# An adaLN block of a two-way Mamba scan and nine experts: downs turned to channel by time, GpSimd's product a slot later, and slots respread

## What is computed

```python
mod = silu(c) @ wmod                       # six rows per batch: sa, ca, ga, sb, cb, gb
h   = layernorm(x) * (1 + ca) + sa
x1  = x + ga * (h + mamba_f(norm(h)) + flip(mamba_b(flip(norm(h)))))
h2  = layernorm(x1) * (1 + cb) + sb
out = x1 + gb * (sum_e w[:, e] * swiglu_e(h2) + swiglu_shared(h2))   # 8 experts, two chosen, softmax of the two

def mamba(xn):                             # 256 inner channels, 16 states
    u, z = split(xn @ Win.T); u = silu(conv4(u)); dt, B, C = project(u)
    h = exp(dt * A) * h + (dt * u) * B     # along time, for each state
    y = sum over states of h * C + u * D
    return (y * silu(z)) @ Wout.T
swiglu_e(t) = (silu(t @ w1) * (t @ w2)) @ w3     # 256 hidden channels
```

## Time and profile before

| | us |
|---|---|
| median of 3 runs | 2398.07 |
| the runs | 2397.0 to 2398.93 |
| the profiled execution's own time | 2398.73 |
| its span, from first to last instruction | 2396.9 |

### The profile page before, as it was taken

One profiled execution on the slowest core, in us unless ns is written; L12 is line 12 of the kernel. 1 busy time (PEld: TensorE's weight loads), 2 busy tenths in 40 slices (PEclk: granted clock), 3 DMA queues, 4 the chain that ended last, 5 costly groups with the idle time before them and its releaser, 6 DMA issues. The chain is left out here.

```text
span 2396.9 us, 31820 instructions
## 1 busy us (share of the span) xinstructions
PE 2026.4 (85%) x9957; PEld 1283.8 (54%) x9957; DVE 2236.7 (93%) x3546; ACT 1504.6 (63%) x2483; POOL 2021.7 (84%) x1334
## 2 busy tenths in 40 slices
PE   6678988879798888988889798888988888897868
PEld 2445655545565555555545465555555555455544
DVE  4999999999999999999999999999999999999962
ACT  4656666676666666666666666666666666666633
POOL 2777989989898998989989898998989889897855
PEclk7688999999999898999999999998999999999999
DMA  5333433433343333334433343343433333343310
GB/s 148 138 137 124 148 130 128 144 130 136 129 147 134 121 138 134 142 126 145 137 127 132 133 142 134 134 141 118 142 134 140 131 133 137 126 138 131 137 59 27
DMA packets 124060, 312.41 MB, mean 130 GB/s; under 512 B 19700, under 2 KB 46308, under 8 KB 123892
## 3 DMA queue, kind: packets, MB, share of 16 engines
q1 hardware_dynamic: 123892, 310.39, 37.5%
HBM read 303.74 MB, written 6.60 MB: 129 GB/s over the span
## 5 line engine op out<-in xcount | busy, mean ns | idle before, releaser
L504 POOL TENSOR_TENSOR bt<-v,bb 128x1024 f32<-128x1024 f32 x511 | 1205.3, 2360 | 93.8 <-DVE psA L942 72.4
L942 DVE TENSOR_TENSOR_SCAN psA<-psA,bt 128x512 f32<-128x512 f32 x1024 | 1198.1, 1217 | 49.3 <-ACT psA L689 42.4
L689 ACT ACTIVATE psA<-dt,aneg 128x512 f32<-128x512 f32 x1024 | 688.4, 688 | 685.2 <-DVE g L952 684.0
L1209 PEld LDWEIGHTS psY<-ident,g 128*128 128x128 f32 x4096 | 491.6, 147 | 504.5 <-DVE g L952 281.2
L1209 PE MATMUL psY<-ident,g 128*128 128x128 f32 x4096 | 590.1, 286 | 198.1 <-DVE g L952 197.9
L952 DVE TENSOR_TENSOR g<-psA,cb 128x512 f32<-128x512 f32 x1024 | 675.0, 679 | 0.0
L602 POOL TENSOR_TENSOR act<-pf,gf 128x512 f32<-128x512 f32 x288 | 366.8, 1274 | 112.2 <-DVE pf L1046 90.7
L1318 PE MATMUL F<-h2T,w 128*128 128x512 f32 x576 | 334.0, 664 | 112.4 <-DVE pf L1046 110.7
L1364 PE MATMUL F<-w,act 128*128 128x128 f32 x2304 | 298.0, 276 | 4.4 <-POOL act L602 3.1
L1364 PEld LDWEIGHTS F<-w,act 128*128 128x128 f32 x2304 | 276.7, 192 | 14.8 <-POOL act L602 11.0
L1225 PE MATMUL psP<-xnT,wcT 128*128 128x512 f32 x496 | 238.6, 604 | 0.0
(11 more groups left out here) (184 smaller groups left out, 1922.5 us busy)
## 6 DMA issues: line engine op xcount, KB each, us to landing
bb<-bc_rows SPq DMA_DIRECT2D x256, 512.0 KB, 3.7
cb<-bc_rows SPq DMA_DIRECT2D x256, 512.0 KB, 3.6
wB<-w_rows SPq DMA_DIRECT2D x80, 256.0 KB, 4.1
x<-in_L_attn_x SPq DMA_DIRECT2D x16, 256.0 KB, 4.4
out_x<-osb SPq DMA_DIRECT2D x16, 256.0 KB, 4.3
modA<-mod_table SPq DMA_DIRECT2D x15, 192.0 KB, 4.1
w<-in_L_ffn_ew SPq DMA_DIRECT2D x2, 1024.0 KB, 7.2
bc_rows<-xd SPq DMA_DIRECT2D x32, 64.0 KB, 3.0
```

What stands on the lines that cost most here:

```text
L504: g.tensor_tensor(bt[:, n % 2, :, :], v[d][:, :, :], bb[:, n // 2 % 2, n % 2, :].unsqueeze(1).broadcast_to([P, NH, T]), ALU.mult).then_inc ...
L689: s.activation(psA[:, half * T:half * T + T], dt_[d][:, half, :], ACT.Exp, scale=aneg[d][:, half, n:n + 1]).then_inc(a_s, 1)
L942: w.tensor_tensor_scan(ah, ah, bt[:, n % 2, half, :][:, order], 0.0, ALU.mult, ALU.add)\
L1209: last = m.matmul(psY[:, half * T + i * P:half * T + i * P + P], g_[:, n % 2, half, i * P:i * P + P], ident[:, :], is_transpose=True, star ...
```

## The change

- **Downs.** Each is now one pair of passes with 512 columns: `w3` is stationary, the activation streams, and the result is channel by time. The order of the experts is 0, 1, shared, 2 to 7. Experts 0 and 1 come out separately; DVE multiplies each by its row of weights and the batch's gate (`product`, slots 14 and 16, into `apart`). The other seven, of which six have scaled inputs, add up in one group in `F2`.
- **End of a batch's experts.** In slot 0 of the body after, ACT copies the group out with the gate (`fold`, ahead of `keep_y`); PE transposes the two products and the folded group into `F1` (`final_turn`, slots 0 and 1); DVE adds the residual (`output`, slot 2). POOL's `output`, ACT's copy, DVE's `expert_sum`, and the two copies of the routing's scores are gone; the routing reads its scores from PSUM.
- **POOL's product** `act` is two slots behind the up instead of one (`ACT_LAG`), into six half buffers instead of three pairs. The ups move to end in slot 29, the downs in slot 31. `make_v` backward moves from slot 14 to 12, the two products of the first layernorm from 7 to 4, the routing weights two slots earlier.
- **Rows of weights**: three buffers, eight rows a batch, written in slot 10 and read from slot 11; in SP's list they come ahead of that slot's rows for the scan.
- **Skip, z.** The forward direction's skip goes into `psY` in slots 8 and 12, and the turns back are plain transposes. The four z parts lie in slots 31, 2, 3 and 5 (PE and ACT) and 0, 3, 4 and 6 (DVE), where they were in 29 to 31 and 2 to 6.

The diff's core:

```diff
-V_SLOT = (30, 14)
-Z_SLOTS, ZS_SLOTS = ((29, 30), (2, 5)), ((30, 31), (6, 6))
+V_SLOT = (30, 12)
+Z_SLOTS = {2: (1, 0), 3: (0, 1), 5: (1, 1)}
+Z_AHEAD_SLOT = 31
+ZS_SLOTS = {0: (0, 0), 3: (1, 0), 4: (0, 1), 6: (1, 1)}
+SKIP_SLOTS = (8, 12)
-UP_SLOTS = [slot for slot in range(7, 28) if slot not in (9, 10, 22)]
-DOWN_SLOTS = [10, 11, 14, 15, 16, 17, 18, 19, 20, 21, 22, 24, 29, 29, 30, 30, 31, 31]
+UP_SLOTS = [slot for slot in range(7, 30) if slot not in (9, 10, 20, 22, 28)]
+DOWN_SLOTS = [10, 11, 15, 16, 17, 18, 21, 24, 25, 26, 27, 28, 28, 29, 29, 30, 31, 31]
+ACTS = 6
+ACT_LAG = 2
-TURN_SLOT, ROWS_SLOT = 13, 14
-XS_SLOTS = {16: 4, 18: 5, 20: 6, 22: 7, 24: 8}
+TURN_SLOT = 10
+XS_SLOTS = {14: 3, 16: 4, 18: 5, 21: 6, 24: 7, 26: 8}
+FOLD_SLOT, FINAL_SLOT, OUT_SLOT = 0, 1, 2
...
-                k = up_at(slot - 1)
+                k = up_at(slot - ACT_LAG)
...
+            def fold(fb):
+
+                act_e.wait_ge(down_s, UPS * fb + UPS)
+                s.activation(foT, F2[:, :], ACT.Copy, scale=modC[:, 2:3]).then_inc(F2_free, 1)
...
+                    if slot == FOLD_SLOT and b >= 2:
+                        fold(b - 2)
                     if slot == 0 and ffn:
                         keep_y(b - 1, 1)
...
+            def product(fb, p):
+
+                n = NX * fb + p
+                dve.wait_ge(down_s, UPS * fb + 2 * p + 2)
+                dve.wait_ge(wB_in[n % ROWS], 16 * (n // ROWS) + 16)
+                wait(dve, fin_s, fb)
+                w.scalar_tensor_tensor(apart[:, p, :], F2[:, :], modC[:, 2:3], wB[:, n % ROWS, :],
+                                       ALU.mult, ALU.mult).then_inc(F2_free, 1)
...
+            def final_turn(fb, slot):
+
+                if slot == FINAL_SLOT - 1:
+                    pe.wait_ge(F1_free, UPS * fb + UPS)
+                    pe.wait_ge(F2_free, FREES * fb + DOWN + APART)
+                    for p in range(APART):
+                        for i in range(NT):
+                            m.matmul(F1[:, i * P:i * P + P], apart[:, p, i * P:i * P + P], ident[:, :],
+                                     is_transpose=True, start=(p == 0 and i == 0), stop=False, skip_group_check=True)
...
-                for e, part in downs_at(slot):
-                    if part == 0:
-                        pe.wait_ge(act_s, 2 * NE * fb + 2 * e + 2)
...
+                for k in downs_at(slot):
+                    if k <= 2 * APART and k % 2 == 0:
+                        pe.wait_ge(F2_free, free + DOWN + k // 2)
+                    pe.wait_ge(act_s, UPS * fb + k + 1)
+                    m.matmul(F2[:, :], w3[:, ORDER[k // 2], k % 2, :], act[:, k % ACTS, :],
+                             start=(k <= 2 * APART and k % 2 == 0), stop=(k < 2 * APART and k % 2 == 1 or k == UPS - 1))\
+                        .then_inc(down_s, 1)
```

More of the change, by code:

```diff
@@ L74, in downs_at, with z_order, row_expert @@
 def downs_at(slot):
-    return [divmod(k, 2) for k, at in enumerate(DOWN_SLOTS) if at == slot]
-ORDER = [NX] + list(range(NX))
+    return [k for k, at in enumerate(DOWN_SLOTS) if at == slot]
+def z_order(b, d, half):
+    return 4 * b + 2 * d + half if b == 0 else 4 * b + d + 2 * half
+def row_expert(idx):
+    return ORDER[idx if idx < APART else idx + 1]
 def adaln_mamba_moe(nc, t, out):
@@ L291, in adaln_mamba_moe @@
         wrow_out = sem("wrow_out")
-        wB_in = [sem(f"wB_in{k}") for k in range(2)]
+        wB_in = [sem(f"wB_in{k}") for k in range(ROWS)]
         xs_s = sem("xs_s")
@@ L433, in body, with scale_row @@
                         sp.dma_start(modG[:, :], row).then_inc(modG_in, 16)
-                    if slot == 0 and not (isinstance(b, int) and b < 2):
+                    if slot == OUT_SLOT + 1 and b >= 2:
                         store(b - 2)
[L437 to L442, removed]
+            def scale_row(fb, idx):
+                n = NX * fb + idx
+                if n >= ROWS:
+                    done, k = divmod(n - ROWS, NX)
+                    if k < APART:
+                        sp.wait_ge(F2_free, FREES * done + DOWN + k + 1)
+                    else:
+                        sp.wait_ge(xs_s, NS * done + k - APART + 1)
+                row = w_dram[row_expert(idx):row_expert(idx) + 1, :].broadcast_to([P, T])
+                sp.dma_start(wB[:, n % ROWS, :], row).then_inc(wB_in[n % ROWS], 16)
             def scales(fb, slot):
-                if slot == ROWS_SLOT:
+                if slot == ROWS_OUT_SLOT:
                     wait(sp, xs_s, NS * fb)
@@ L449, in scales @@
                     sp.dma_start(w_dram, wtsT[:, :]).then_inc(wrow_out, 16)
[L450 to L456, removed]
+                for idx, at in ROW_SLOTS.items():
+                    if slot == at:
+                        if idx == 0:
+                            sp.wait_ge(wrow_out, 16 * fb + 16)
+                        scale_row(fb, idx)
             def early(b, scan, ffn, last):
@@ L460, in early @@
                     fb = b - 1
[L461 to L466, removed]
+                    wait(sp, F2_free, FREES * fb)
+                    with nc.allow_non_contiguous_dma(reason="three columns"):
+                        sp.dma_start(modC[:, :], mod_dram[bass.ds(fb, 1), 3 * D:6 * D]
+                                     .rearrange("a (k p) -> p (a k)", p=P)).then_inc(modC_in, 16)
                 if scan and not last:
@@ L861, in body @@
                         keep_y(b, 0)
+                    if ffn and slot == GATE_SLOT + 1:
+                        act_e.wait_ge(gate_s, GATES * (b - 1) + GATE_D)
+                        s.activation(ge[:, :], gd[:, :], ACT.Exp).then_inc(ge_s, 1)
                     if ffn:
@@ L885, in _ @@
             passes(act_e, body)
+            fold(NB - 1)
         @block.vector
@@ L1082, in ffn_side @@
                     gate(fb)
-                if slot == GATE_SLOT + 3:
+                if slot == GATE_SLOT + 1:
                     gate_weights(fb)
+                if slot in PRODUCT_SLOTS:
+                    product(fb, PRODUCT_SLOTS.index(slot))
             def side(b, slot, prep_b, prep_f, post_f):
@@ L1164, in body @@
                         ffn_side(b - 1, slot)
-                        expert_sum(b - 1, slot)
+                    if slot == OUT_SLOT and b >= 2:
+                        output(b - 2)
                     if scan_ and slot - POST_F_SLOT in (0, 1):
@@ L1169, in _ @@
             passes(dve, body)
+            output(NB - 1)
         @block.tensor
@@ L1263, in side @@
                     wait(pe, pP_free, post_piece(b, half))
-                    skip_and_turn(psP, 0, half).then_inc(pP_full, 1)
+                    turn(psP, 0, half, False).then_inc(pP_full, 1)
+                if post_f and slot in SKIP_SLOTS:
+                    skip(0, SKIP_SLOTS.index(slot))
                 if prep_f is not None:
@@ L1403, in body @@
                         sum_y(step - 1, 4 * b - 2, N - 1)
+                    if b >= 2 and slot in (FINAL_SLOT - 1, FINAL_SLOT):
+                        final_turn(b - 2, slot)
+                    if slot == Z_AHEAD_SLOT and scan_ and not last:
+                        project_z(b + 1, 0, 0)
                     if ffn:
```

271 lines of the change are left out of this document (120 added, 151 removed).

## The result

The changed kernel takes 2449.1 us in the median (2444.9 to 2449.9) beside 2398.5 for the kernel before on the same chip: 1.021 times as long, with an interval of 1.019 to 1.023. The forecast was 2417.5 and the range 2350 to 2430. Slower was right; the size was not: +50.6 us where +19.5 was forecast.

What follows compares the result with a forecast made beforehand. DVE, busy 93% of the span, was taken to set the pace, with POOL's queue and PE's lower clock limiting slots 29 to 1. 14 x 3.9 - 15 x 2.1 - 0.6 - 3 = +19.5 us: 2417.5 us, range 2350 to 2430.

Steps and rivals of the forecast that it cites:

- 14 wraps, slot 29 to slot 1: Batch end into the next body: POOL's late last products delay slot 1, 21.6 us instead of 17.7, +3.9 each.
- 15 stretches, slots 1 to 28: Slots 1 to 28 of each period: less DVE work, a gain of 2.1 us, between 2.4 and 1.8.
- body 0 and the first wrap: Body 0 and the wrap into body 1, which have no experts: about -0.6 us together.
- the tail: Kernel's end: turns halved, cheaper finish after the last down, shorter waits of first downs; -3 us, between -6 and 0.
- the eight turns: PE's turns behind the last down in the wrap: 1.29 us at the lower clock, instead of 1.04.
- Rival A: In the wrap PE keeps its full rate, +2.7 us each: 2401 us, 2385 to 2408 with bounds; chance 0.26.
- the term for new waits: Slots 1 to 28, from slot 10's product behind `make_dt` and moved `make_v` and skip: 0.3 us a period, 0 to 0.6.
- the three quartets: Groups of four small `facc` instructions on DVE, removed in each period: 3 x 1.03 = 3.1 us saved.
- I cost that at 0: PE's load rising in slots 25 to 27: no cost, or some tenths a period if PE is late there.
- Rival C: PE's lower level lasts into slots 0 and 1, 1 to 2.5 us a wrap more: 2431 to 2452; chance 0.11.
- Rival B: POOL's last-product chain does not bind the wrap, DVE alone sets the pace, -0.6 a wrap: 2350 to 2355; chance 0.23.

Runs made afterwards that it cites:

- The three together: Changed kernel with POOL's product one slot behind the up, tanh ahead of `keep_y` in slot 16, and downs off slots 25 to 27: 2353.7 us, 0.982 times the kernel before.

## Why the prediction was right and wrong

| term | forecast | measured in the timelines |
|---|---|---|
| 14 wraps, slot 29 to slot 1 | 14 x +3.9 = +54.6 | 14 x +4.4 = +61.6 |
| 15 stretches, slots 1 to 28 | 15 x -2.1 = -31.5 | 15 x -0.3 = -4.6 |
| body 0 and the first wrap | -0.6 | -3.2 |
| the tail | -3 | -3.3 |
| sum | +19.5 | +50.5 |

Of the -3.2, 1.6 lie ahead of DVE's first scan, which starts 45.2 to 49.4 us into the span in the runs here; so that part can be scatter.

**The wrap** came as it was worked out, queue by queue: slot 0 at 14.04 (14.0), the product's end at 16.45 (16.50), the last down at 2.08 at a granted clock of 0.50, slot 1 released by ACT behind `keep_y`, `sum_y` and that down. The size was 0.5 a wrap short because I took the eight turns at 1.29 from the earlier trace rows; they took 1.91, as PE was still at the lower level for all of them. I had misread that row: its turns start at 1379.13, the granted clock is 0.50 up to 1379.50 but 1.00 in the window from 1379.70 to 1384.00, so most of that row is at the full rate. (My own terms add up to 21.53, not 21.6.) **Rival A**, the full rate, is what the run with PE kept busy shows: 20.3 us from slot 29 to slot 1 in eleven of the wraps, +2.6 where A has +2.7.

**Slots 1 to 28** is the step that failed: the term for new waits, 0.3 and between 0 and 0.6, measured 2.6 a period. In sum none of it is in slots 9 to 13, where I looked for it: slots 11 and 12 have new waits, 9 and 13 are shorter by as much, and the five take 22.0 us in the mean as before. Its parts: 1.22 in slot 16, 0.92 in slots 27 and 28, and 0.46 in slot 1. Together 15 x 2.14 + 14 x 0.46 = 38.5 us; without them the stretch would have come to (-4.6 - 38.5) / 15 = -2.9 a period, better than the -2.1 that I took (slots 7 and 18 became 0.3 and 0.4 shorter, which I had not counted). The three together show it: 122.0 us in the mean where the kernel before has 124.9.

Slot 16: I took each of the three quartets at 1.03 us from the earlier trace rows, as if DVE were bound by its own work in slot 15. The row behind it, `pf` of slot 16 (1250.09), which I did not follow back, ends a chain over PE and ACT that was just as long. The gain of that quartet, taken at 1.03, was 0.

Slots 27 and 28: "I cost that at 0; if PE is late there, it costs some tenths a period" names the place, and what came was 0.92. I argued from ACT's work. PE was full there: `sum_y` 0.87, up 1.8, down 0.95 and dt piece 1.05 make 4.7 us, from start to start on PE's timeline of slot 27, against a slot of 4.24.

**Rival C**, the lower level reaching into slots 0 and 1, was there by 0.46 us in slot 1, and in the run with the down behind `sum_y` by 2.8. That the measured time lies among C's 2431 to 2452 is luck: C's cause has 14 x 0.46 = 6.4 us of it. **Rival B** did not happen in this kernel. Its time, 2350 to 2355, is that of the kernel with the three chains taken away, 2353.7, but by two misses that cancel: a wrap there is 0.2 longer than before and not 0.6 shorter, and slots 1 to 28 are 2.9 shorter and not 2.1 to 2.4. What does hold of B is that the saved DVE work turned into time, once nothing else was late.

The Trainium skill (Perfetto Trace Analysis, "Identifying the Most-Contended Engine") sends one to the busiest engine first. Here that engine was relieved of 36 us, and the time rose by 50.6; the saving showed only after the order of the other engines had been mended.

## What to carry to other kernels

Work removed from the busiest engine is worth nothing where another chain just as long runs beside it: follow the next instruction's releaser back before the gain is counted. A delay of an engine with time to spare was free here in the middle of the loop and dear at its end, where its last result stands in an in-order queue ahead of what the next iteration needs; count the whole queue there, on every engine. Where PE must wait for a late operand, look up in a trace at which clock it works behind such a wait, and price everything that stands behind it by that clock. Here it was the lower one in all 14 wraps behind the waits of 4.3 to 4.7 us, and in nine of ten wraps, for a part of the down and the turns at least, behind those of 2.24 us in the run with POOL's order changed.

## What the hardware showed that I had not expected

After 4.67 us without work PE ran at a granted clock of 0.50 (1.2 GHz) for the down, the eight turns and part of the turns back, some 4.5 us; between 1351.20 and 1353.00 the windows view has 0.94. Five matmuls of no use in the gap, 4.45 us of PE work, kept the full 2.4 GHz (1.00 in the window shown) and made the kernel 28.9 us faster, without a change to the rest of its work or to its order.

The Trainium skill (TensorE: Matmul & The Clock Gate, Part 1) puts the penalty of the ramp from the lower clock, where it speaks of a kernel's first matmuls, under 1% of a typical span. Here the lower level costs 28.9 of 2449.1 us, 1.2%, since it comes back in each of the 14 wraps.
